# A post-norm attention and ternary-FFN layer: a new hand-written order of the instruction queues, PSUM banks open to every stage, and a last pair whose FFN runs one batch at a time

## The chip, the cores and the metric

The kernel runs on one core of a Trainium2 chip. The metric is device time in microseconds (us) of that core. Each engine (TensorE = PE, VectorE = DVE, ScalarE = ACT, GpSimd = POOL, and SyncE = SP, which issues the DMAs) runs its own list of instructions strictly in the order in which they are written. Engines meet only at semaphores.

## The reference

For 32 batches of 256 tokens of width 128 (fp32 throughout):

```
Q, K, V = x Wq^T, x Wk^T, x Wv^T            # 8 heads; Q, K of width 64, V of width 128 per head
A = softmax(Q K^T)                          # no scale, over the 256 keys, per batch and head
x1 = layernorm(x + sum over heads of A V)
h = silu((x1 w1^T) s1) * ((x1 w2^T) s2)     # 128 -> 512, w ternary times 8
h = gelu((h h1^T) s3); h = gelu((h h2^T) s4)   # 512 -> 512, twice, exact gelu
out = layernorm(x1 + (h w3^T) s5)           # 512 -> 128
```

## The kernel before, in words

**Precision.** Each fp32 operand is split into a high and a low part of the PE's faster fp32r type; a product is three matmuls (high*high, high*low, low*high). The high part is a copy (ACT `copy`, DVE or POOL `tensor_copy`), the low part a subtraction (`minus`, L196). The FFN weights are ternary, so their low parts are zero and two matmuls are enough. That isn't assumed: all low parts of the FFN weights are reduced to one flag, PE reads it (L1101) and branches to a body with or without the third matmul. The traced run takes the body without it.

**Tiling.** Two batches make a pair of 512 tokens; there are 16 pairs. One matmul writes up to one PSUM bank of 512 fp32 columns; there are 8 banks. A pair needs:

- `query_or_key(i, t)`, t = 0..7, and `values(i, n)`, n = 0..7: three 512-wide matmuls each. ACT copies the high part out of the bank (`t_high`, `v_high`), DVE subtracts the low part (`t_low`, `v_low`).
- `scores(i, g)`, g = 0..7: two heads of one batch, 12 matmuls of 64 rows and 256 columns, of which two at a time run side by side. DVE takes the row maximum (`row_max`, L600), ACT the exponential (`exp`, L383, two instructions and two reads of the sum for each of 16 blocks u), DVE the reciprocal, POOL normalizes (`norm`, L248).
- `turn_prob(i, u)`, u = 0..15: four 128x128 transposes (L852) of block u; then `pt_high` on ACT, `pt_low` on DVE; then `times_v(i, u)`, six 256-wide matmuls into bank 7. After the eight blocks of a batch come `acc_copy` (ACT), `turn_attention` (two transposes), `res_add`, `stats`, `norm1` (DVE) and `rstd` (POOL).
- FFN: `turn_x1` (four transposes), `layer1_z1`/`layer1_z2`, o = 0..3 (two 512-wide matmuls each), `tanh` (ACT), `silu` and `gate` (DVE); `layer2`, `layer3` (32 512-wide matmuls each, in halves of four per output), each output through `gelu2`/`gelu3` (ACT), `high` and `low`; `layer4` (8 matmuls), `yt_copy`, `turn_y`, `y_add`, `stats2`, `rstd2`, `norm2`, store.

**Staging.** `cycle(k)` (L989) is the PE's order of one period. It is written out by hand and mixes three pairs: it ends the FFN of pair k-2, does most of the attention of pair k and the FFN of pair k-1, and starts Q, K, V and scores of pair k+1. ACT, DVE and POOL have hand-written loops over k with the same period. Cycles 0 to 18 all run the same text; where a pair doesn't exist the call does nothing. Cycle 0 comes after a short prologue, and the flag is read after it.

**Banks.** Every stage has fixed banks (L22 to L32): Q, K, V in banks 2 and 4, all transposes of probabilities in bank 3, FFN in 0 and 1, scores in 5 and 6, the sum over heads in 7. Before PE writes a bank again it waits for the last reader; those waits are the extra tuples of each call in `cycle`.

**The head.** SP issues x^T of pair 0, all weights, the residual of pair 0 and then (L216) x^T of pair 1, which needs the buffer `xt_in` free. ACT and DVE split Wq, Wk, Wv; POOL splits the 11 pieces of the FFN weights between the `norm`s of cycle 0 (`split_weights`), DVE reduces each (`largest_lo`, L558), PE turns the maximum (`turn_flag`), DVE makes the flag (L570).

**The tail.** The FFN of pair 15 runs in cycles 16 and 17, where no other pair is left.

**ACT's function tables.** The exponential and tanh are in one table, gelu in another; a copy works with both. Where the order goes from `exp` or `tanh` to `gelu` or back, an ACT_TABLE_LOAD stands in ACT's queue. Per pair the order of before has four groups of gelu: `gelu3(k-2,3)` with `gelu3(k-2,2)` before it, `gelu2(0,1)`, `gelu2(2,3)`, `gelu3(0,1)`.

The change also touches every function that names a bank.

Of the kernel before, what the change touches and what calls it, by code (L numbers as in the profile page):

```python
# [21 lines left out]
T_BANK = (2, 2, 4, 4, 2, 4, 2, 2)  # L22
V_BANK = (4, 2, 4, 4, 2, 4, 2, 4)
TURN_BANK = (3, 3, 3, 3, 3, 3, 3, 3, 3, 3, 3, 3, 3, 3, 3, 3)
AT_BANK = (2, 4)
X1T_BANK = 1
Z1_BANK = (0, 0, 0, 1)
Z2_BANK = (1, 1, 0, 0)
L2_BANK = (1, 0, 1, 0)
L3_BANK = (1, 0, 1, 0)  # L30
L4_BANK = 1
YT_BANK = 1  # L32

T_FIRST = {0: 0, 1: 1, 2: 2, 3: 4, 4: 0, 5: 1, 6: 2}
V_FIRST = {0: 4, 1: 0, 2: 1, 3: 2}
# [5 lines left out]
def need(eng, sem, value):  # L41

    if value > 0:
        eng.wait_ge(sem, value)


def layer_kernel(nc, x, x_t, wq_t, wk_t, wv_t, w1_t, w2_t, h1_t, h2_t, w3_t, scales_t, out):
# [8 lines left out]
    VT = TT * H * D // TOK  # L56

# [6 lines left out]
    def after(i, per, n):  # L64

        return min(i * per + n, PAIRS * per)

    with ExitStack() as ctx:
# [38 lines left out]
        with ExitStack() as early:  # L107
# [26 lines left out]
        sc = bank[5:7]  # L134
# [3 lines left out]
        (s_wqk, s_wv, s_wf, s_ident, s_wqk_hi, s_wqk_lo, s_wv_hi, s_wv_lo, s_wf_hi, s_wf_lo, s_lomax,  # L138
         s_flagt, s_flag, s_zero, s_scales, s_halves, s_held) = (sem(n) for n in (
            "wqk_in", "wv_in", "wf_in", "ident_made", "wqk_hi", "wqk_lo", "wv_hi", "wv_lo", "wf_hi", "wf_lo",  # L140
            "lomax_made", "flag_turned", "flag_made", "zeroed", "scales_in", "halves_ready", "held"))
# [19 lines left out]
        WF = [(w1_hi[:, :], w1_lo[:, :], w1_in[:, :]), (w2_hi[:, :], w2_lo[:, :], w2_in[:, :])]  # L161
        WF += [(h1_hi[:, c, :], h1_lo[:, c, :], h1_in[:, c, :]) for c in range(KC)]
        WF += [(h2_hi[:, c, :], h2_lo[:, c, :], h2_in[:, c, :]) for c in range(KC)]
        WF += [(w3_hi[:, :, :], w3_lo[:, :, :], w3_in[:, :, :])]
        NWF = len(WF)
# [7 lines left out]

        def v_cols(n):
            t, half = V_ORDER[n]
            return t, slice(half * TOK, (half + 1) * TOK)

        def t_bank(i, t):
            return bank[T_FIRST[t] if i == 0 and t in T_FIRST else T_BANK[t]]

        def v_bank(i, n):
            return bank[V_FIRST[n] if i == 0 and n in V_FIRST else V_BANK[n]]

# [3 lines left out]
        def slot(i, u, ring):  # L187
            return (i * J + u) % ring
# [13 lines left out]
        def _(sp):  # L202
            sp.dma_start(xt_in[:, :], x_t[0]).then_inc(s_xin, 16)
            sp.dma_start(wq_in[:, :], wq_t).then_inc(s_wqk, 16)
            sp.dma_start(wk_in[:, :], wk_t).then_inc(s_wqk, 16)
            sp.dma_start(wv_in[:, :], wv_t).then_inc(s_wv, 16)
            sp.dma_start(scales[:, :], scales_t).then_inc(s_scales, 16)
            sp.dma_start(w1_in[:, :], w1_t).then_inc(s_wf, 16)
            sp.dma_start(w2_in[:, :], w2_t).then_inc(s_wf, 16)
            sp.dma_start(h1_in[:, :, :], h1_t.rearrange("(c p) o -> p c o", p=P)).then_inc(s_wf, 16)  # L210
            sp.dma_start(h2_in[:, :, :], h2_t.rearrange("(c p) o -> p c o", p=P)).then_inc(s_wf, 16)
            sp.dma_start(w3_in[:, :, :], w3_t.rearrange("(c p) o -> p c o", p=P)).then_inc(s_wf, 16)
# [17 lines left out]
            for k in range(-3, PAIRS + 3):  # L230
                load_res(k)
                load_xt(k + 3)
                store(k - 2)
            sp.wait_ge(s_yfree, 16 * PAIRS)

        @block.gpsimd
        def _(pool):
# [26 lines left out]
            def split_weights(k, g):  # L264
                if k == 0:
                    hi, lo, w = WF[g]
                    if g == 0:
                        pool.wait_ge(s_wf, 16 * 5)
                    nc.gpsimd.tensor_copy(hi, w).then_inc(s_wf_hi, 1)
                    pool.wait_ge(s_wf_hi, g + 1)  # L270
                    minus(nc.gpsimd, lo, w, hi).then_inc(s_wf_lo, 1)

            def low(f, layer, c):
                if there(f):
                    full, hi, lo, _, s_hi, s_lo = LAYER[layer]
                    pool.wait_ge(s_hi[c], f + 1)
                    minus(nc.gpsimd, lo[:, c, :], full[:, c % 2, :], hi[:, c, :]).then_inc(s_lo[c], 1)

# [14 lines left out]

            def norm2(f):
# [6 lines left out]

            norm(0, 0)
            norm(0, 1)
            norm(0, 2)

            for k in range(PAIRS + 3):
                low(k - 2, 3, 2)
                rstd1_of(k - 1, 1)
                norm(k, 3)
                split_weights(k, 0)  # L310
                norm(k, 4)
                split_weights(k, 1)
                norm(k, 5)
                split_weights(k, 2)
                norm(k, 6)
                split_weights(k, 3)
                norm(k, 7)
                split_weights(k, 4)
                low(k - 1, 1, 0)
                norm(k, 8)  # L320
                split_weights(k, 5)
                norm(k, 9)
                split_weights(k, 6)
                low(k - 1, 1, 1)
                norm(k, 10)
                split_weights(k, 7)
                low(k - 1, 1, 2)
                norm(k, 11)
                split_weights(k, 8)
                norm(k, 12)  # L330
                split_weights(k, 9)
                low(k - 1, 2, 0)
                low(k - 1, 2, 1)
                norm(k, 13)
                split_weights(k, 10)
                low(k - 1, 2, 2)
                norm(k, 14)
                rstd2_of(k - 2)
                norm(k, 15)
                low(k - 1, 3, 0)  # L340
                norm(k + 1, 0)
                rstd1_of(k, 0)
                norm(k + 1, 1)
                norm(k + 1, 2)

        @block.scalar
        def _(act):
# [4 lines left out]
            def split_wv(g):  # L352
                cols = slice(g * TOK, (g + 1) * TOK)
                if g == 0:
                    act.wait_ge(s_wv, 16)
# [788 lines left out]
```

## Time and profile before

| | |
|---|---|
| median of 3 runs | 1031.53 us (1029.31 to 1032.75) |
| the profiled execution | 1031.28 us, of which the span from first to last instruction is 1029.4 us |
| PE busy | 984.3 us (96%) |
| PE weight load busy | 816.5 us (79%) |
| ACT busy | 859.1 us (83%) |
| DVE busy | 827.1 us (80%) |
| POOL busy | 513.0 us (50%) |
| mean granted TensorE clock | 0.98 of full speed |

The profile shows one execution. A matmul's row starts when it starts; its end is modelled and overlaps the next one's start, so the pace of PE is read from start to start, not from the durations. "Idle before" is the idle time of an engine ahead of a group, with the instruction that ended it.

### The profile page before, as it was taken

What the parts mean: (1) busy time and instruction counts of PE and PEld (TensorE: products, weight loads), DVE (VectorE), ACT (ScalarE), POOL (GpSimd) and SP (SyncE); (2) the same over time, 40 slices, a digit from 0 to 9 for tenths busy, and PEclk for the clock granted to TensorE, in tenths of its full rate; (3) what the DMA queues carried; (4) which work ended last, traced back from release to release, by engine and by line L of the source; (5) the groups of instructions that cost most, each with busy time, mean ns of one, the idle gap of its engine ahead of it and who ended that gap; (6) DMA issues with size and microseconds to landing.
All of it is one profiled execution on the core that took longest, in us unless ns stands there. A gap on an engine that the chain in (4) does not pass through costs nothing.

```text
span 1029.4 us, 19535 instructions
## 1 busy us (share of the span) xinstructions
PE 984.3 (96%) x6465; PEld 816.5 (79%) x6465; DVE 827.1 (80%) x1827; ACT 859.1 (83%) x1992; POOL 513.0 (50%) x509
## 2 busy tenths in 40 slices
PE   4887999999999999999999999999999999999976
PEld 3676888888888888888888888888888888888844
DVE  4695778887888988788898878889887888878754
ACT  5574998989899898989989898998989899898632
POOL 1591545544455554545555454555545454554623
PEclk9898999999999999999999999999999999999978
DMA  5000000000100000010000001000000100000000
GB/s 184 11 3 21 2 11 12 21 11 2 31 2 22 12 21 11 1 32 2 21 12 21 12 2 32 2 22 11 22 11 2 32 1 12 11 12 11 12 0 21
DMA packets 21749, 17.81 MB, mean 17 GB/s; under 512 B 1040, under 2 KB 17936, under 8 KB 21648
## 3 DMA queue, kind: packets, MB, share of 16 engines
q1 hardware_dynamic: 21648, 16.53, 5.3%
q8 instruction: 56, 0.92, 0.4%
q14 instruction: 45, 0.37, 0.1%
HBM read 12.33 MB, written 4.19 MB: 16 GB/s over the span
## 4 chain that ended last, share of the span: by engine, by line
PE 91%; DVE 4%; ACT 2%; issue 2%; DMA 0%; POOLq 0%; SPq 0%; DVEq 0%; POOL 0%; ACTq 0%
PE bank L852 13%; PE bank L958 13%; PE bank L959 13%; PE bank L846 12%; PE bank L848 11%; PE bank L847 11%; PE bank L891 11%; PE bank L938 3%; PE bank L939 3%; ACT prob L383 1%; DVE pt_lo L196 1%; DMA wk_in<-in_wk_t 0%; DVE neg_max L600 0%; DVE t_lo L196 0%; DVE v_lo L196 0%
## 5 line engine op out<-in xcount | busy, mean ns | idle before, releaser
L248 POOL TENSOR_TENSOR prob<-prob,inv_total 128x512 f32<-128x512 f32 x256 | 267.8, 1057 | 185.0 <-DVE inv_total L606 185.0
L383 ACT ACTIVATE prob<-bank,neg_max 128x256 f32<-128x256 f32 x512 | 237.9, 480 | 4.1 <-DVE neg_max L600 3.4
L196 DVE TENSOR_TENSOR pt_lo<-bank,pt_hi 128x512 fp32r<-128x512 f32 x256 | 175.4, 685 | 46.3 <-ACT pt_hi L199 41.8
L199 ACT ACTIVATE pt_hi<-bank 128x512 fp32r<-128x512 f32 x256 | 154.2, 602 | 66.9 <-PE bank L852 64.5
L600 DVE TENSOR_REDUCE neg_max<-bank 128x2 f32<-128x512 f32 x256 | 171.4, 681 | 24.7 <-PE bank L891 24.7
L852 PE MATMUL bank<-ident,prob 128*128 128x128 f32 x1024 | 157.7, 277 | 7.2 <-issue 4.7
L852 PEld LDWEIGHTS bank<-ident,prob 128*128 128x128 f32 x1024 | 120.9, 141 | 39.9 <-issue 9.6
L846 PE MATMUL bank<-pt_hi,v_hi 128*128 128x256 f32 x512 | 151.9, 297 | 0.0
L848 PE MATMUL bank<-pt_hi,v_lo 128*128 128x256 f32 x512 | 145.3, 284 | 0.0
L847 PE MATMUL bank<-pt_lo,v_hi 128*128 128x256 f32 x512 | 145.3, 284 | 0.0
L196 POOL TENSOR_TENSOR even_lo<-gelus,even_hi 128x512 fp32r<-128x512 f32 x48 | 61.8, 1288 | 103.7 <-DVE even_hi L678 103.7
L383 ACT ACTIVATION_READ_ACCUMULATOR prob<-bank,neg_max 128x1 f32 x512 | 108.3, 212 | 0.0
L958 PE MATMUL bank<-odd_hi,h_hi 128*128 128x512 f32 x256 | 107.0, 418 | 0.0
L958 PE MATMUL bank<-even_hi,h_hi 128*128 128x512 f32 x256 | 105.6, 412 | 0.2 <-DVE even_lo L196 0.2
L196 DVE TENSOR_TENSOR v_lo<-bank,v_hi 128x512 fp32r<-128x512 f32 x128 | 86.9, 679 | 23.1 <-ACT v_hi L199 23.1
L196 DVE TENSOR_TENSOR t_lo<-bank,t_hi 128x512 fp32r<-128x512 f32 x128 | 86.9, 680 | 19.5 <-ACT t_hi L199 19.5
L847 PEld LDWEIGHTS bank<-pt_lo,v_hi 128*128 128x128 f32 x512 | 98.3, 192 | 4.3
L959 PE MATMUL bank<-odd_lo,h_hi 128*128 128x512 f32 x256 | 101.5, 397 | 0.0
L846 PEld LDWEIGHTS bank<-pt_hi,v_hi 128*128 128x128 f32 x512 | 98.1, 192 | 4.0
L959 PE MATMUL bank<-even_lo,h_hi 128*128 128x512 f32 x256 | 101.1, 395 | 0.0
L848 PEld LDWEIGHTS bank<-pt_hi,v_lo 128*128 128x128 f32 x512 | 98.3, 192 | 0.0
L199 ACT ACTIVATE v_hi<-bank 128x512 fp32r<-128x512 f32 x128 | 77.2, 603 | 23.7 <-PE bank L848 23.7
(101 smaller groups left out, 2357.2 us busy)
## 6 DMA issues: line engine op xcount, KB each, us to landing
xt_in<-in_x_t SPq DMA_DIRECT2D x16, 256.0 KB, 2.7
res<-in_x SPq DMA_DIRECT2D x16, 256.0 KB, 2.8
out_x<-y SPq DMA_DIRECT2D x16, 256.0 KB, 2.3
h_in<-in_h_t SPq DMA_DIRECT2D x2, 1024.0 KB, 9.2
w_in<-in_w_t SPq DMA_DIRECT2D x3, 256.0 KB, 5.9
wv_in<-in_wv_t SPq DMA_DIRECT2D x1, 512.0 KB, 5.9
wq_in<-in_wq_t SPq DMA_DIRECT2D x1, 256.0 KB, 3.1
wk_in<-in_wk_t SPq DMA_DIRECT2D x1, 256.0 KB, 5.1
```

The lines of the kernel that those rows point to most:

```text
L196: return eng.tensor_tensor(dst, src, hi.bitcast(F32), ALU.subtract)
L199: return nc.scalar.activation(dst, src, ACT.Copy)
L248: nc.gpsimd.tensor_tensor(prob[:, s, :, :], prob[:, s, :, :], inv_total[:, u, :].unsqueeze(2).to_broadcast([P, NT, N]), ALU.mult).then_inc ...
L383: last = nc.scalar.activation(prob[:, slot(i, u, RING), nt, :], sc[u % 2][:, nt * N:(nt + 1) * N], ACT.Exp, bias=neg_max[:, u, nt:nt + 1], ...
L600: nc.vector.tensor_reduce(neg_max[:, u, :], sc[u % 2].rearrange("p (t m) -> p t m", m=N), AX.X, ALU.max, negate=True).then_inc(s_max, 1)
L846: mm(dst, w_hi, m_hi, start=start, stop=False)
L847: mm(dst, w_hi, m_lo, start=False, stop=False)
L848: return mm(dst, w_lo, m_hi, start=False, stop=stop)
L852: last = turn(dst[:, n * P:(n + 1) * P], b, ident[:, :])
L891: ends.append(mm(sc[n][:, nt * N:(nt + 1) * N], left[rows, t, q], right[rows, t + 1, m], start=(term == 0), stop=(term == 2)))
L958: mm(dst, w_hi[:, c, cols], m_hi[:, c, :], start=begins, stop=False)
L959: last = mm(dst, w_hi[:, c, cols], m_lo[:, c, :], start=False, stop=ends and not with_lo)
```

## The change

1. **Banks.** The tables of fixed banks are replaced by tables in which every stage may use banks 0 to 6; scores get a pair of banks for each g (`SC_BANK`) in place of banks 5 and 6. Tables `*_OTHER` override them for the pairs 0, 1, 13, 14 and 15. `scores` waits for named readers in place of the fixed wait on `exp` of the scores before.
2. **The order of a pair.** `cycle(k)` and the loops of ACT, DVE and POOL are written in a new order, used for k = 1 to 14. The work of a pair is the same, but for three moves: the copy `xt_high(k+2)` goes from ACT to POOL, `high(k-1,2,0)` from DVE to ACT, `low(k-1,2,1)` from POOL to DVE. All eight `query_or_key` of pair k+1 and its `scores` 0 to 2 are now in cycle k. On ACT the gelus of a pair stand in two groups.
3. **The first pairs.** Prologue and cycle 0 become one list of its own on each engine. Wq and Wk are loaded in two parts each (128 and 384 columns), with a semaphore for each load; the splits are spread over ACT, DVE and POOL; POOL splits the FFN weights earlier. On ACT `xt_high(1)` stands after `t_high(0,3)`. The flag is read when `turn_prob(0,14)` has been issued.
4. **The last pair.** `last` replaces cycles 15 to 18. It runs the FFN of pair 15 as two batches of 256 columns each: every 512-wide matmul becomes two 256-wide ones, every evacuation two of half the width, with semaphores `s_ends` of their own. The chunks of layers 2 to 4 are interleaved between the batches. Store and final norm go by batch as well.

```diff
-T_BANK = (2, 2, 4, 4, 2, 4, 2, 2)
-TURN_BANK = (3, 3, 3, 3, 3, 3, 3, 3, 3, 3, 3, 3, 3, 3, 3, 3)
-Z1_BANK = (0, 0, 0, 1)
-L2_BANK = (1, 0, 1, 0)
+T_BANK = (2, 0, 3, 0, 1, 5, 6, 3)
+SC_BANK = ((4, 2), (5, 6), (3, 1), (3, 5), (1, 6), (1, 3), (3, 2), (1, 5))
+TURN_BANK = (2, 0, 4, 2, 4, 4, 1, 6, 0, 3, 6, 3, 0, 4, 0, 6)
+AT_BANK = (1, 0)
+L2_BANK = (2, 4, 0, 1)
...
             sp.dma_start(xt_in[:, :], x_t[0]).then_inc(s_xin, 16)
-            sp.dma_start(wq_in[:, :], wq_t).then_inc(s_wqk, 16)
-            sp.dma_start(wk_in[:, :], wk_t).then_inc(s_wqk, 16)
+            sp.dma_start(wq_in[:, A], wq_t[:, A]).then_inc(loads["wqa"], 16)
+            sp.dma_start(wk_in[:, A], wk_t[:, A]).then_inc(loads["wka"], 16)
+            sp.dma_start(wq_in[:, B_], wq_t[:, B_]).then_inc(loads["wqb"], 16)
+            sp.dma_start(wk_in[:, B_], wk_t[:, B_]).then_inc(loads["wkb"], 16)
...
# ACT, first pairs
+            weight_high("wka")
+            t_high(0, 0)
+            t_high(0, 1)
+            t_high(0, 2)
+            weight_high("wv1")
+            t_high(0, 3)
+            xt_high(1)
+            weight_high(0)
+            t_high(0, 4)
+            t_high(0, 5)
+            exp(0, 0)
+            exp(0, 1)
...
# ACT, the gelus of a pair in the loop over k
+                gelu3(k - 2, 2)
+                gelu3(k - 2, 3)
...
+                gelu2(k - 1, 0)
+                high(k - 1, 2, 0)
+                pt_high(k, 11)
+                gelu2(k - 1, 1)
+                gelu2(k - 1, 2)
+                t_high(k + 1, 5)
+                t_high(k + 1, 6)
+                t_high(k + 1, 7)
+                gelu2(k - 1, 3)
...
+                gelu3(k - 1, 0)
+                gelu3(k - 1, 1)
+                v_high(k + 1, 3)
...
# PE, one stretch of cycle(k)
+                turn_prob(k, 9, (s_t_lo, k + 1, H, 3))
+                query_or_key(k + 1, 4, (s_exp, k, J, 15))
+                turn_prob(k, 10, (s_v_lo, k + 1, VT, 3))
+                layer2(k - 1, 2, 0, w, (s_t_lo, k + 1, H, 4))
                 layer2(k - 1, 0, 1, w)
+                turn_attention(k, 0, (s_t_lo, k + 1, H, 5))
+                turn_prob(k, 11, (s_pt_lo, k, J, 10))
                 layer2(k - 1, 1, 1, w)
+                layer2(k - 1, 3, 0, w, (s_radd, k, 2, 1))
+                layer2(k - 1, 2, 1, w)
+                query_or_key(k + 1, 5, (s_exp, k, J, 16))
+                scores(k + 1, 0, (s_gelu2, k - 1, KC, 2), (s_gelu2, k - 1, KC, 1))
...
# a chunk of a layer of the last pair, one batch
+            def quarter(b, c, dst, w_hi, w_lo, m_hi, m_lo, cols, with_lo, prior, s_out, readers):
+                m = of_batch(b)
+                free(*readers)
+                pe.wait_ge(*half_done(prior, 1, b, c))
+                begins, ends = c == 0, c == KC - 1
+                mm(dst, w_hi[:, c, cols], m_hi[:, c, m], start=begins, stop=False)
+                last = mm(dst, w_hi[:, c, cols], m_lo[:, c, m], start=False, stop=ends and not with_lo)
...
# PE, the end of last(w)
+                times_v(15, 13)
+                turn_x1_half(0, (s_yadd, 14, 1, 1))
+                times_v(15, 14)
+                times_v(15, 15)
+                layer1_z1_half(0, 0, w, (s_yt, 14, 1, 1))
+                turn_attention(15, 1, (s_x1t_lo, 15, 1, 1))
+                layer1_z1_half(0, 1, w, (s_radd, 15, 2, 1))
+                layer1_z2_half(0, 0, w, (s_acc, 15, 2, 2))
...
+                turn_y_half(0, (s_gelu3, 15, KC, 2))
+                layer4_half(1, 2, w)
+                layer4_half(1, 3, w)
+                turn_y_half(1, (s_gelu3, 15, KC, 5))
```

## Rows read from the trace of the kernel before

**Rows 1.** Stretches: length, busy time (instructions) by engine, PE clock, DMA share, GB/s.

```profile
0.00:40.00 40.00, 22.56 (x101) 16.43 (x102) 19.53 (x35) 19.63 (x48) 9.50 (x16) 0.87 0.38 125
40.00:77.90 37.90, 33.90 (x259) 27.33 (x257) 34.20 (x75) 28.30 (x85) 31.62 (x34) 1.00 0.02 8
82.20:144.92 62.72, 60.66 (x388) 50.67 (x388) 44.88 (x94) 50.88 (x121) 27.76 (x27) 0.93 0.04 10
398.49:458.65 60.16, 60.16 (x406) 50.50 (x406) 50.83 (x114) 54.33 (x125) 30.85 (x31) 1.00 0.05 14
927.00:980.90 53.90, 53.18 (x360) 44.78 (x359) 43.12 (x98) 41.42 (x96) 28.67 (x28) 1.00 0.04 11
980.90:1029.40 48.50, 31.86 (x112) 20.68 (x110) 24.14 (x57) 12.92 (x20) 14.30 (x14) 0.79 0.04 11
```

**Rows 2.** Timeline of PE in one pair: start, duration, engine, line, tiles, count.

```profile
402.59 0.39 PE L939 MATMUL bank<-x1t_lo,w_hi 128*128 128x512 f32 x1
402.82 0.60 PE L852 MATMUL bank<-ident,prob 128*128 128x128 f32 x4
403.17 0.48 PE L938 MATMUL bank<-x1t_hi,w_hi 128*128 128x512 f32 x1
403.49 0.40 PE L939 MATMUL bank<-x1t_lo,w_hi 128*128 128x512 f32 x1
403.81 0.39 PE L891 MATMUL bank<-t_hi 64*128 64x256 f32 x2
404.03 0.28 PE L891 MATMUL bank<-t_lo,t_hi 64*128 64x256 f32 x2
...
404.51 0.28 PE L891 MATMUL bank<-t_hi,t_lo 64*128 64x256 f32 x2
404.72 0.50 PE L938 MATMUL bank<-x1t_hi,w_hi 128*128 128x512 f32 x1
405.06 0.39 PE L939 MATMUL bank<-x1t_lo,w_hi 128*128 128x512 f32 x1
...
406.31 0.28 PE L847 MATMUL bank<-pt_lo,v_hi 128*128 128x256 f32 x1
406.43 0.28 PE L848 MATMUL bank<-pt_hi,v_lo 128*128 128x256 f32 x1
...
409.74 0.63 PE L852 MATMUL bank<-ident,prob 128*128 128x128 f32 x4
410.30 0.39 PE L891 MATMUL bank<-t_hi 64*128 64x256 f32 x2
```

**Rows 3.** Groups by line in that pair: count, busy, mean ns, idle before.

```profile
L383 ACT ACT_TABLE_LOAD x4 | 5.1, 1283 | 0.1
L383 ACT ACTIVATE prob<-bank,neg_max 128x256 f32<-128x256 f32 x32 | 14.9, 481 | 0.0
L199 ACT ACTIVATE pt_hi<-bank 128x512 fp32r<-128x512 f32 x16 | 9.6, 603 | 3.2 <-PE bank L852 3.1
L196 DVE TENSOR_TENSOR pt_lo<-bank,pt_hi 128x512 fp32r<-128x512 f32 x17 | 11.7, 686 | 2.6 <-ACT pt_hi L199 2.3
```

**Rows 4.** Timeline of the head; in brackets, idle before and what ended it.

```profile
8.79 0.79 PE L846 MATMUL bank<-xt_hi,wq_hi 128*128 128x512 f32 x1 [8.79 <-DVE wk_lo L196]
8.91 21.33 SPq L218 DMA_DIRECT2D xt_in<-in_x_t  x2
...
82.23 1.09 PE L852 MATMUL bank<-ident,prob 128*128 128x128 f32 x4 [4.72 <-issue]
```

**Rows 5.** The loads of `xt_in` in the first 60 us, from issue to landing.

```profile
DMA to landing us min/median/max: 2.7/2.9/8.3
```

**Rows 6.** Timeline of the tail, in the same form.

```profile
982.22 0.42 DVE L621 TENSOR_TENSOR res<-bank,res 128x256 f32<-128x256 f32 x1 [0.69 <-PE bank L852]
...
1021.29 0.63 PE L852 MATMUL bank<-ident,yt 128*128 128x128 f32 x4 [0.87 <-ACT yt L446]
1021.96 0.69 DVE L690 TENSOR_TENSOR y<-bank,x 128x512 f32<-128x512 f32 x1 [2.33 <-PE bank L852]
```

More of the change, by code:

```diff
@@ L172, in layer_kernel, with half_done, of_batch @@
         }
+        s_ends = {n: (sems(f"end{n}_hi"), sems(f"end{n}_lo")) for n in (1, 2, 3)}
+        def half_done(layer, low, b, c):
+            return (s_ends[layer][low][c], 1) if b else (LAYER[layer][4 + low][c], LAST + 1)
+        def of_batch(b):
+            return slice(b * N, (b + 1) * N)
         def v_cols(n):
@@ L467, in _ @@
+            exp(0, 4)
             v_high(0, 2)
+            exp(0, 5)
             v_high(0, 3)
-            xt_high(1)
-            for k in range(PAIRS + 3):
+            pt_high(0, 1)
+            pt_high(0, 2)
+            exp(0, 6)
+            exp(0, 7)
+            pt_high(0, 3)
+            t_high(1, 0)
+            exp(0, 8)
+            v_high(0, 4)
+            t_high(1, 1)
+            v_high(0, 5)
+            exp(0, 9)
+            pt_high(0, 4)
+            pt_high(0, 5)
+            v_high(0, 6)
@@ new lines, in _ @@
+            xt_high(2)
+            v_high(0, 7)
+            exp(0, 10)
+            exp(0, 11)
+            exp(0, 12)
+            pt_high(0, 6)
+            t_high(1, 2)
+            t_high(1, 3)
+            exp(0, 13)
+            pt_high(0, 7)
+            pt_high(0, 8)
+            exp(0, 14)
+            v_high(1, 0)
+            t_high(1, 4)
+            weight_high(6)
+            exp(0, 15)
+            pt_high(0, 9)
+            pt_high(0, 10)
+            acc_copy(0, 0)
+            exp(1, 0)
@@ L472, in _ @@
+            v_high(1, 1)
+            exp(1, 1)
+            t_high(1, 5)
+            pt_high(0, 11)
+            pt_high(0, 12)
+            v_high(1, 2)
+            t_high(1, 6)
+            exp(1, 2)
+            exp(1, 3)
+            pt_high(0, 13)
+            t_high(1, 7)
+            pt_high(0, 14)
+            exp(1, 4)
+            pt_high(0, 15)
+            v_high(1, 3)
+            for k in range(1, LAST):
                 pt_high(k, 0)
+                gelu3(k - 2, 2)
                 gelu3(k - 2, 3)
-                t_high(k, 7)
@@ new lines, in _ @@
+            row_max(1, 1)
+            pt_low(0, 10)
+            inverse(0, 14)
+            largest_low(6)
+            v_low(1, 1)
+            largest_low(7)
+            t_low(1, 5)
+            pt_low(0, 11)
+            pt_low(0, 12)
+            largest_low(8)
+            t_low(1, 6)
+            v_low(1, 2)
+            row_max(1, 2)
+            largest_low(9)
+            row_max(1, 3)
+            largest_low(10)
+            res_add(0, 0)
+            flag_by_partition()
+            halves()
@@ new lines, in _ @@
+            high(14, 1, 3)
+            low(14, 1, 2)
+            inverse(15, 13)
+            row_max(15, 15)
+            stats2_of(13)
+            pt_low(15, 9)
+            high(14, 2, 0)
+            low(14, 2, 0)
+            low(14, 2, 1)
+            v_low(15, 6)
+            low(14, 2, 2)
+            high(14, 2, 3)
+            low(14, 2, 3)
+            v_low(15, 7)
+            inverse(15, 14)
+            pt_low(15, 10)
+            res_add(15, 0)
+            high(14, 3, 0)
+            inverse(15, 15)
@@ L1100, in _ @@
+            times_v(0, 11)
+            scores(1, 1, (s_pt_lo, 0, J, 13), (s_t_lo, 1, H, 6))
+            scores(1, 2, (s_exp, 1, J, 2), (s_t_lo, 1, H, 7))
+            turn_attention(0, 0, (s_v_lo, 1, VT, 3))
+            values(1, 3, (s_pt_lo, 0, J, 12))
+            times_v(0, 12)
+            query_or_key(1, 7, (s_exp, 1, J, 3))
+            turn_flag((s_radd, 0, 2, 1))
+            turn_prob(0, 14, (s_exp, 1, J, 4))
+            pe.wait_ge(s_halves, 2)
             pe.wait_ge(s_flag, 1)
```

1454 lines of the change are left out of this document (1085 added, 369 removed).

## Prediction

> **What bounds the kernel now.** I read the table of stretches first, then PE's own timeline, then ACT's groups, then the two ends of the span.
>
> In the middle PE is the bound and nothing else comes near. From 398.49 to 458.65, one period of 60.16 us, PE is busy for all of it, ACT for 54.33, DVE for 50.83 and POOL for 30.85 [rows 1]. PE's waits in the middle (120 to 930) are an empty list. So the middle can only get shorter if the same matmuls take PE less time. The ends are different. Ahead of 77.9 DVE is busy for 19.53 + 34.20 = 53.7 us and ACT for 47.9; PE is idle until 8.79, and the clock of the first 40 us is 0.87 [rows 1, 4]. The last 48.5 us hold 31.86 us of PE at a clock of 0.79 [rows 1].
>
> Score block 0 of a pair is transposed once a period, and I cut the span there. Those places are 144.92 for pair 2 and 927.00 for pair 15. The span is then: PE's work until the flag, which ends at 82.23 - 4.72 = 77.5; an idle stretch of 4.7 for reading the flag and branching [rows 4]; 62.7 to the start of pair 2; 13 x 60.16 = 782.1; a tail of 53.9 + 48.5 = 102.4 [rows 1]. Sum 1029.4. The profiled execution took 1031.28, 1.9 more than its span, and the median of the runs is 1031.5.
>
> **PE's price list.** Start to start, a 512-wide matmul takes 0.23 (402.59 to 402.82), a 256-wide one 0.12 (406.31 to 406.43, and a side-by-side pair of scores likewise), four transposes 0.35 (402.82 to 403.17). The matmul behind transposes takes 0.32, 0.09 more. Going into scores costs 0.09 on the matmul before and 0.10 on the first scores (403.49, 403.81, 404.03), 0.19; leaving them costs 0.09 and 0.11 (404.51, 404.72, 405.06), 0.20. Transposes ahead of scores take 0.56 in place of 0.35 (409.74 to 410.30), with the 0.10 that is 0.31 [rows 2]. Scores into transposes isn't in the rows: between 0.09 and 0.20, I take 0.15.
>
> A pair has 136 512-wide matmuls, 96 + 48 slots of 256, and 76 transposes: at 0.232, 0.119 and 0.089 that is 31.6 + 17.1 + 6.8 = 55.5. Before, 16 matmuls follow transposes (1.4); scores are entered six times from a matmul and twice from transposes (1.76) and left five times to a matmul and three times to transposes (1.45). Sum 60.1, against 60.16 measured: the list closes, and there is no hidden stall in the middle.
>
> **The new order of a pair.** It has the same instructions on PE. 16 matmuls still follow transposes. Scores are entered six times from a matmul, once from transposes, and once from scores (`scores(k+1,1)` and `(k+1,2)` are neighbours); left five times to a matmul and twice to transposes. That is 1.45 + 1.30 against 1.76 + 1.45: 0.46 less, so 59.7.
>
> Would PE now wait? Gelus stand in two groups, not four, so four of the eight table loads go (the four to the exponential in rows 3, and as many to gelu), 4 x 1.283 = 5.1 us of ACT per pair [rows 3]; the copy that goes to POOL and the one that comes from DVE cancel (0.6 each). ACT falls to about 49 of 59.7. DVE trades a copy for a subtraction (0.686), about 51. POOL gets a copy (0.6) and loses a subtraction. By the orders, the PE time between `scores` and the transposes of its blocks is 13.6 us at the least, before 13.2; between a transpose and its `times_v` 3.8, before 2.4. The tightest place is bank 1: `turn_attention(k,0)` writes it and `layer2(k-1,3,0)` takes it again after 1.4 us (0.36 + 1.02), when `res_add` has read it. DVE has `pt_low(k,10)` ahead of `res_add`, and ACT has `pt_high(9)`, `t_high(4)`, `exp(15)`, `pt_high(10)` ahead of that: from the end of `turn_prob(k,9)` 0.6 + 0.6 + 0.96 + 0.6 on ACT [rows 3], 0.69 and 0.42 on DVE [rows 3, 6] and some 0.3 for semaphores, 4.2. PE's own work until there is 0.79 + 0.36 + 1.02 + 0.93 + 0.18 + 0.36 + 1.02 = 4.7. It fits by 0.5. I add 0.1 per pair for places that don't: 59.8, at the least 59.6, at the most 62.3 (a miss of one exp, one copy and one subtraction, 2.3, on top of 60). 13 pairs give 777.4, 4.7 less than before.
>
> **The head.** The small first parts of Wq and Wk should let PE start near 5.5 in place of 8.79 [rows 4]: x^T comes first as before, a copy and a subtraction follow, and 64 KB come sooner than 256. I count nothing for it. ACT now has `xt_high(1)` fifth in its list, ahead of the first exponentials. x^T of pair 1 was issued at 8.91 behind all weights and landed 8.3 later, at 17.2 [rows 4, 5]; nothing moves it up. So ACT stands still from about 11 to 17 and DVE behind it. Before, `exp(0,0)` began before 17; now it begins near 19.5. What is won is the rest: by the flag ACT has to do about 42.5 us (before 47.9; it has three `pt_high`, two `exp` and three weight copies fewer), some 3 of them before 17; DVE about 52 (before 53.7), some 7 before 17. POOL, busy for 31.6 of 37.9 us up to the flag [rows 1] since it began on the weights only in cycle 0, now begins them at once. DVE is the bound: 17 + 45 = 62 if it never waits. From 40 to 77.9 it waited 10% of the time [rows 1]; with 5.5 us of waits PE's work until the flag ends at 67.5. It can't be under 62; if the blocks of ACT and POOL cost as much as the old order's waits did it is 77.5. I take 67.5. The 4.7 us of the branch stay. Cycle 1 was 62.7 for 56.7 us of PE work by the list, the rest being a cold clock (0.93, rows 1) and one more gap; the new cycle 1 has 55.8 with the one transposition group before it, so 61.8. Pair 2 starts at 67.5 + 4.7 + 61.8 = 134.0, 10.9 earlier.
>
> **The tail.** From the transposes of block 0 of pair 15, PE has 76.0 us of work in the old order and 76.4 in the new (a 256-wide matmul costs 0.119, half of 0.232, so the halves add 0.5). Behind PE's last transposes comes the chain of norm and store: 1021.29 to 1029.4, 8.1 us [rows 6]; for half the tokens I take 6 (between 5 and 8). Before, 102.4 - 76.0 - 8.1 = 18.3 us were stalls and a cold clock, all but one of them in the FFN of pair 15, which ran alone. Now batch 0 starts its FFN when 14 of 16 `times_v` are out, and each batch hides the other's evacuations. A chain remains for batch 1: `turn_attention`, residual, norm, `turn_x1` take some 7 us, as before, but beside batch 0; then four outputs per layer, each with gelu, copy, subtraction, 2.5 to 3 us a layer for three layers. Against it stand 24 us of PE work. I take 8.5 us of stalls (between 4 and 15) in place of 18.3. Tail 76.4 + 6 + 8.5 = 91, 11.4 less.
>
> The Trainium skill, "TensorE: Matmul & The Clock Gate", section "Back-to-back issue gap", speaks against the halves: in a stream of weight load and matmul pairs it gives 81 ns at 128 columns and 131 ns at 512, so that halving the columns doesn't halve the time; an estimate from it for 256 is 98, which would make the 88 FFN matmuls of the last pair 5.7 us dearer. This case's trace doesn't agree: 0.12 at 256 columns and 0.23 at 512 [rows 2], 0.5 us for all of them.
>
> **Sum.** 67.5 + 4.7 + 61.8 + 777.4 + 91 = 1002.4 us of span, with 1.9 around it 1004.3; against the median (0.3 above the profiled execution) 1004.5. I say 1004, 2.7% faster.
>
> **Rivals.**
> - *The middle gains nothing.* Small bank waits eat the 0.46 a pair and 0.1 to 0.6 more. For it: margins of 0.5 us, 69 bank reuses per pair, none of which the old trace shows. Against: ACT gets 5 us of air. 13 x 0.4 to 1.0 more: 1009 to 1017. 17%.
> - *The head gains nothing.* The wait for x^T of pair 1 on ACT costs more than POOL's early start gives, and the flag comes at 77 as before. For it: the 6 us in which ACT stands. 1014. 13%.
> - *Both ends are better than I think.* DVE waits under 3 us behind 17, the tail has under 5 us of stalls: 995. 17%.
> - *The other side: one wait per pair in the middle.* The DVE queue is late at bank 1 because `exp(k,15)` or a table load falls ahead of `pt_high(k,10)`; the stall of PE comes once each pair. It decides from (1031.5 - 1004.5) / 14 = 1.9 us a pair; with 2.4 (one load, one copy and the subtraction late) it is 1004.5 + 14 x 2.4 = 1038. For it: strict queues, margin 0.5. Against: distances to the transposes grew nearly everywhere. 7%.
> - *The order doesn't do what it says*, because the clock stays low in the head: it is in the numbers above. 1%.
> - My forecast, 999 to 1009: 45%.
>
> **How the numbers follow.** The forecast, the better ends and most of the first two rivals lie between 991 and 1018; what is left out is the other side and their far tails, 2 in 10. About 0.3% is what a measurement of this kernel can tell. Faster by that: 0.46 + 0.17 + 0.13 + 0.14 = 0.90; within it 0.03; slower 0.07.
>
> **What would show it.** Right: a period of 59.6 to 60.0 between the transposes of block 0, PE busy throughout, four table loads a pair; ACT idle ahead of `xt_high(1)` until 17; the flag read near 67; the last transposes of PE 85 us behind those of block 0 of pair 15. Wrong: a releaser of PE in the middle with a total over 10 us; the flag later than 75; a tail over 97.

## The result and the profile after

The changed kernel takes 1008.36 us (median of 4 runs, 1007.14 to 1008.57); the kernel before took 1030.72 in the same series (4 runs, 1029.31 to 1032.75). The ratio is 0.9774, with a 95% interval of 0.9762 to 0.9786: 2.3% faster. The forecast was 1004 with a range of 991 to 1018.

I cut the span after at the same places as before: where PE's work ends at the flag, where it goes on, the transposes of score block 0 of pair 2 (now at 129.81) and of pair 15 (now at 918.83). The table of stretches of the changed kernel, in the columns of [rows 1]:

```profile
0.00:64.30 64.30, 50.97 (x357) 42.26 (x357) 48.75 (x101) 44.02 (x129) 39.69 (x47) 0.92 0.25 79
64.30:69.49 5.19, 0.00 (x1) 0.03 (x1) 3.86 (x13) 1.70 (x6) 5.11 (x5) 0.72 0.18 43
69.49:129.81 60.32, 59.33 (x389) 50.76 (x390) 47.46 (x97) 47.27 (x119) 23.80 (x26) 0.94 0.04 12
129.81:918.83 789.02, 777.32 (x5253) 658.34 (x5252) 712.82 (x1469) 648.48 (x1574) 383.80 (x390) 1.00 0.05 14
918.83:1006.50 87.67, 79.16 (x557) 69.86 (x555) 70.01 (x171) 55.96 (x133) 49.76 (x55) 0.97 0.05 13
```

| part | before | forecast | after |
|---|---|---|---|
| PE's work until the flag | 77.5 | 67.5 | 64.3 |
| idle ahead of the branch's program | 4.7 | 4.7 | 5.2 |
| to the start of pair 2 | 62.7 | 61.8 | 60.3 |
| 13 pairs | 782.1 | 777.4 | 789.0 |
| tail | 102.4 | 91 | 87.7 |
| span | 1029.4 | 1002.4 | 1006.5 |

Both ends gave more than forecast, 29.8 us with the idle time and cycle 1 in place of 22.3. The middle, which was to give 4.7, took 6.9. Together that is the 22.9 by which the spans differ. Its 13 periods are 60.69 us each in place of 60.16 [rows 1], although the 777.32 us of PE's work in them is 59.79 a pair. The missing 0.90 has a single place. The waits of the middle, where the list of PE was empty before (one row: who waited <- for what, us in total, times, longest):

```profile
PE bank L1455 <- DVE x L982: 11.7, 13, 0.9
```

It is `turn_x1`, which turns the normed tokens of the pair before for the FFN. First what DVE and POOL did ahead of it, then PE's own row:

```profile
141.40 0.71 POOL L369 TENSOR_TENSOR rstd<-var_eps,minus_half 128x2 f32<-128x2 f32 x1
141.59 0.67 DVE L260 TENSOR_TENSOR pt_lo<-bank,pt_hi 128x512 fp32r<-128x512 f32 x1
142.09 3.04 POOL L327 TENSOR_TENSOR prob<-prob,inv_total 128x512 f32<-128x512 f32 x3
142.17 3.29 DVE L982 TENSOR_SCALAR x<-res,mv,rstd 128x128 f32<-128x128 f32 x4
145.52 0.66 PE L1455 MATMUL bank<-ident,x 128*128 128x128 f32 x4 [0.90 <-DVE x L982]
```

The four operations that write `x` (`norm1` of both batches) take 3.29 us, and beside the first three of them POOL runs three norms of `prob` back to back; the fourth begins when POOL is done and takes 0.33 again. In the kernel before, the same four stood in a gap between two norms:

```profile
454.51 2.04 POOL L248 TENSOR_TENSOR prob<-prob,inv_total 128x512 f32<-128x512 f32 x2
...
456.48 1.11 DVE L645 TENSOR_SCALAR x<-res,mv,rstd 128x128 f32<-128x128 f32 x4
...
458.34 1.04 POOL L248 TENSOR_TENSOR prob<-prob,inv_total 128x512 f32<-128x512 f32 x1 [1.79 <-DVE inv_total L606]
```

Over the middle, one line for each kernel, before and then after (shortest, median and longest of 52, in ns):

```profile
L645 DVE TENSOR_SCALAR x<-res,mv,rstd x52: 333/342/448, 155.7 to 878.4; 128x128 f32<-128x128 f32 x52
```

```profile
L982 DVE TENSOR_SCALAR x<-res,mv,rstd x52: 333/1056/1079, 142.2 to 873.4; 128x128 f32<-128x128 f32 x52
```

So the same instruction on the same shapes is three times as long. The trace of before held the effect already, at a place where nobody waited: four operations of `norm2`, of the same shape and also from SBUF to SBUF (the on-chip memory that isn't PSUM), start at 200.76, and the last of them, the only one beside a norm of POOL (from 201.40), takes 1.06 us where the others take 0.34. Over the middle of before:

```profile
L697 DVE TENSOR_SCALAR y<-y,mv,rstd x52: 331/337/1062, 200.8 to 922.8; 128x128 f32<-128x128 f32 x52
```

The length of `x` is what the page's chain of waits shows too: its line "DVE x L982 5%" is the only one of DVE in it above 1%, because the chain runs through `x` once a pair.

The head, in the form of [rows 4]. ACT stands in front of `xt_high(1)`, PE waits for a subtraction that is behind it, and the branch comes at 64:

```profile
17.96 0.63 ACT L263 ACTIVATE xt_hi<-xt_in 128x512 fp32r<-128x512 f32 x1 [7.21 <-DMA xt_in<-in_x_t]
20.41 0.58 PE L1498 MATMUL bank<-t_hi 64*128 64x256 f32 x2 [7.40 <-DVE t_lo L260]
63.68 0.62 PE L1455 MATMUL bank<-ident,prob 128*128 128x128 f32 x4
69.49 1.94 PE L1455 MATMUL bank<-ident,prob 128*128 128x128 f32 x8 [5.20 <-POOL prob L327]
```

The tail, answering to [rows 6]. The last transposes of PE start at 1000.52, 81.7 behind those of block 0 of pair 15, and the stores of the two halves are issued at 1002.86 and after:

```profile
974.50 0.44 PE L1455 MATMUL bank<-ident,at 128*128 128x128 f32 x2 [0.24 <-ACT at L263]
977.57 0.36 PE L1627 MATMUL bank<-odd_hi,h_hi 128*128 128x256 f32 x1 [0.98 <-DVE odd_lo L260]
1000.52 0.44 PE L1455 MATMUL bank<-ident,yt 128*128 128x128 f32 x2 [0.57 <-ACT yt L639]
1002.86 1.78 SPq L299 DMA_DIRECT2D out_x<-y  x2
```

### The profile page after: what moved, and what is told of

The parts are those of the page before. It is cut to its first block, busy times and chain, and to the rows that moved or that the text cites. A ratio compares the mean times of both kernels' runs of the same rounds, so it can differ in the third digit from the quotient of the medians.

```text
span 1006.5 us, 19738 instructions
## 1 busy us (share of the span) xinstructions
PE 966.8 (96%) x6553; PEld 821.3 (82%) x6553; DVE 882.9 (88%) x1846; ACT 797.4 (79%) x1958; POOL 502.2 (50%) x520
## 4 chain that ended last, share of the span: by engine, by line
PE 86%; DVE 8%; issue 2%; POOL 1%; DMA 1%; SPq 1%; ACT 1%; POOLq 0%; DVEq 0%; ACTq 0%
PE bank L1567 13%; PE bank L1568 12%; PE bank L1455 12%; PE bank L1449 11%; PE bank L1451 11%; PE bank L1450 10%; PE bank L1498 10%; DVE x L982 5%; PE bank L1547 3%; PE bank L1548 3%; DVE y L1027 1%; DMA xt_in<-in_x_t 1%; DVE res L958 1%; DVE stats L964 1%; PE bank L1627 1%
## 5 line engine op out<-in xcount | busy, mean ns | idle before, releaser
L327 POOL TENSOR_TENSOR prob<-prob,inv_total 128x512 f32<-128x512 f32 x256 | 272.3, 1072 | 179.2 <-DVE inv_total L943 179.2
L1449 PE MATMUL bank<-pt_hi,v_hi 128*128 128x256 f32 x512 | 158.2, 309 | 0.0
L1455 PEld LDWEIGHTS bank<-ident,prob 128*128 128x128 f32 x1024 | 123.3, 142 | 30.1 <-POOL prob L327 5.4
L260 POOL TENSOR_TENSOR odd_lo<-gated,odd_hi 128x512 fp32r<-128x512 f32 (+1 forms) x50 | 62.2, 1244 | 83.5 <-ACT odd_hi L263 82.9
L1567 PE MATMUL bank<-even_hi,h_hi 128*128 128x512 f32 x240 | 98.8, 412 | 0.0
L1567 PE MATMUL bank<-odd_hi,h_hi 128*128 128x512 f32 x240 | 97.3, 405 | 0.0
L263 ACT ACTIVATE t_hi<-bank 128x512 fp32r<-128x512 f32 x128 | 76.3, 598 | 23.7 <-PE bank L1451 19.5
L1568 PE MATMUL bank<-odd_lo,h_hi 128*128 128x512 f32 x240 | 94.8, 395 | 0.0
```

Of the source, the lines that this page charges most:

```text
L260: return eng.tensor_tensor(dst, src, hi.bitcast(F32), ALU.subtract)
L263: return nc.scalar.activation(dst, src, ACT.Copy)
L327: nc.gpsimd.tensor_tensor(prob[:, s, :, :], prob[:, s, :, :], inv_total[:, u, :].unsqueeze(2).to_broadcast([P, NT, N]), ALU.mult).then_inc ...
L1449: mm(dst, w_hi, m_hi, start=start, stop=False)
L1455: last = turn(dst[:, n * P:(n + 1) * P], b, ident[:, :])
L1567: mm(dst, w_hi[:, c, cols], m_hi[:, c, :], start=begins, stop=False)
```

## Experiments

All are edits of the changed kernel (1008.36). Each was timed against the kernel before; times below are medians, ratios are to the kernel before with 95% intervals. For comparison, the changed kernel has 0.9774 [0.9762, 0.9786].

**POOL keeps still while `x` is written (e1_pool_waits)**

```diff
                 rstd1_of(k - 1, 1)
+                hold(pool, s_x1, 2 * k)
                 norm(k, 5)
```

> One wait more on POOL: behind rstd1 of batch 1 it waits for the two norm1 of that pair (four tensor_scalars of x) before it goes on with the norm of score block 5. Theory A (the four tensor_scalars of x are slow because POOL's norms of prob run beside them): L982 falls from a mean of 1056 ns to about 340, x is ready some 2.9 us sooner, PE's 0.90 us wait for x ahead of turn_x1 is gone from every pair, the period goes from 60.69 to about 59.8; 13 periods and the last pair give about 12 us: 996 (994 to 999). Rival B (they are slow by themselves, in the place or the operands that the new order gives them): L982 stays above 1000 ns, the wait of PE stays 0.9, 1008. Rival C (A's gain is given back because POOL's norms come some 1.5 us later and the transposes of block 5 wait for them): L982 at 340 ns, but a new wait of PE for POOL of about 1 us per pair, 1005 to 1010.

Measured: 995.71 us (994.88 to 996.74), ratio 0.9653 [0.9637, 0.9669]. The stretch from block 0 of pair 2 to that of pair 15 is wholly PE's work, 59.75 a period, and `x` is fast again:

```profile
128.71:905.44 776.73, 776.73 (x5253) 659.29 (x5252) 687.22 (x1469) 648.01 (x1574) 384.77 (x390) 1.00 0.05 14
```

```profile
L983 DVE TENSOR_SCALAR x<-res,mv,rstd x52: 334/339/344, 141.1 to 858.9; 128x128 f32<-128x128 f32 x52
```

```profile
141.09 1.10 DVE L983 TENSOR_SCALAR x<-res,mv,rstd 128x128 f32<-128x128 f32 x4
142.12 0.68 DVE L260 TENSOR_TENSOR pt_lo<-bank,pt_hi 128x512 fp32r<-128x512 f32 x1
142.37 3.04 POOL L327 TENSOR_TENSOR prob<-prob,inv_total 128x512 f32<-128x512 f32 x3 [1.34 <-DVE x L983]
```

POOL waits 1.34 us for `x` and then takes the same 3.04 for its three norms, and nobody waits for it in turn: PE has no wait at all in the middle. Theory A holds, B and C fall. One added wait is worth 12.7 us.

**The first half of `norm1` earlier (e2_norm1_split)**

```diff
                 y_add(k - 2)
+                norm1(k - 1, 0)
                 inverse(k, 5)
                 inverse(k, 6)
                 inverse(k, 7)
                 pt_low(k, 2)
-                norm1(k - 1, 0)
                 norm1(k - 1, 1)
```

> Only the order of DVE is changed: norm1 of batch 0 comes directly behind the addition into y, ahead of three reciprocals and a subtraction (pt_low of block 2). Theory A (the length of the x operations beside POOL is the cause, not their place): L982 stays between 700 and 1056 ns, but two of the four are out before, so x is ready 1 to 2 us sooner; PE's wait for x shrinks to 0 to 0.3 and the time to 996 to 1001, if the delayed subtraction of block 2 doesn't become a wait of its own (then a new row of PE for pt_lo, and 1003 to 1010). Rival B (x is late because rstd of batch 1 is late on POOL, wherever norm1 of batch 0 stands): the wait stays 0.9, 1008.

Measured: 996.63 us (995.95 to 998.17), ratio 0.9664 [0.9648, 0.968]. PE's wait for `x` is gone from all pairs of the middle. The median of the `x` operations is lower than the 700 to 1056 that I had given, because most of the first two now fall ahead of POOL's norms; only the longest is what it was:

```profile
L982 DVE TENSOR_SCALAR x<-res,mv,rstd x52: 340/462/1079, 140.9 to 860.3; 128x128 f32<-128x128 f32 x52
```

The time agrees with theory A, the length of the operations doesn't; rival B falls. Two edits on two engines that both take operations of `x` from beside POOL's norms give the same 12 us.

**Eight table loads a pair in place of four (e5_more_loads, e10_loads_in_gaps)**

The first puts them between the gelus, the second where ACT waited longest:

```diff
+            def extra_switch():
+                nc.scalar.activation(junk[:, :], scales[:, 0:1], ACT.Exp)
...
                 gelu3(k - 2, 2)
+                extra_switch()
                 gelu3(k - 2, 3)
...
                 gelu2(k - 1, 1)
+                extra_switch()
                 gelu2(k - 1, 2)
```

```diff
+            def extra_switch():
+                nc.scalar.activation(junk[:, :], scales[:, 0:1], ACT.Gelu)
...
                 v_high(k, 4)
+                extra_switch()
                 x1t_high(k - 1)
...
                 exp(k + 1, 2)
+                extra_switch()
                 pt_high(k, 13)
```

> Each of the two groups of gelus in a pair is cut in two by an exponential of one column into a scratch tile, so that ACT loads its tables eight times per pair as before the change, not four. Theory A (in the middle PE bounds, ACT's 49 us of a 60.7 us period leave room, and the four loads that the change saves are worth nothing by themselves): ACT busy near 54 us per period, period within 0.3 of 60.7, 1008 to 1012. Rival B (grouping the gelus is what keeps the ring of banks moving): PE gets waits for gelu2, gelu3 or the next exponentials of 1 to 3 us per pair, 1022 to 1048.

> The same four extra table loads per pair as in e5_more_loads, but placed where ACT of the changed kernel waits longest: a gelu of one column into the scratch tile ahead of x1t_high (ACT waits 1.38 us there) and ahead of pt_high of block 13 (it waits 1.07 there and 0.58 at the next copy). Theory A (the 33 us of e5_more_loads come from its place, 2.8 us between two gelus with scores' blocks queued behind; ACT's total has room, 55 of 60.7): the lump overhangs each gap by about 1.4, which the distances of 3 us and more between a copy and its reader take up; 1008 to 1016. Rival B (a lump of 2.8 us on ACT costs PE about its overhang wherever it stands, so the four loads that the grouping saves are worth 1 to 3 us per pair): 1022 to 1048.

Measured: 1041.41 us (1040.0 to 1043.11), ratio 1.0097 [1.008, 1.0113], and 1039.63 us (1039.44 to 1040.68), ratio 1.0092 [1.0077, 1.0108]. Theory A was wrong both times, by 29 and 24 us from the upper end of its ranges, and B was right. ACT is busy for 55.37 and 55.27 us of a period, with over 7 us to spare, and yet both periods are long, 63.19 and 62.97. PE's waits in the middle, of the first and then of the second:

```profile
PE bank L1504 <- ACT prob L539: 15.1, 12, 1.5
PE bank L1504 <- DVE t_lo L261: 13.4, 12, 1.1
PE bank L1461 <- DVE x L988: 10.8, 12, 0.9
```

```profile
PE bank L1461 <- ACT prob L539: 11.8, 24, 0.6
PE bank L1461 <- DVE x L988: 10.8, 12, 0.9
PE bank L1573 <- DVE pt_lo L261: 6.0, 12, 0.5
```

Besides the wait for `x` that was there already, a lump of 1.28 + 0.2 + 1.28 us makes PE wait 1.1 and 1.3 on average at two places when it stands between the gelus, and 0.5 at each of three places when it stands in ACT's widest gaps. (In the second, 0.8 us of the longer period isn't in these rows, because a matmul's modelled end hides the first part of a wait. Read from start to start beside the changed kernel, in one period, PE loses 0.73, 0.57 and 0.74 us at the three places and 0.06 to 0.08 at each of three matmuls behind the first, 2.2 of the 2.3.) So this order, which all but fills PE, has no distance left for two loads in one lump at these places, where ACT's total would have had room. That grouping the gelus is a condition for the rest of the change isn't shown by this: the order of before has eight loads a pair, one by one, and PE waits for nothing in its middle. A new order with the loads spread like that was not run.

**The last pair like all others (e4_old_tail)**

```diff
-            load_res(15)
-            store(13)
-            store(14)
-            store_half(0)
-            store_half(1)
...
-                for k in range(1, LAST):
+                for k in range(1, PAIRS + 2):
                     cycle(k, False)
-                last(False)
```

The lists of the last pair go from all engines, and with them the bank tables of their own from pair 13 on; counts are cut off at the last pair as they were before the change.

> The last pair goes as all others do: pair 15 in the steady order, then its layers for both batches at once, one store; the head and the order of the middle stay. Theory A (the tail's 14.7 us come from running the last layers one batch at a time, so that one batch's matmuls cover the other's gelus, copies and subtractions): the tail from the transposes of score block 0 of pair 15 is 100 to 103 us again in place of 87.7, and the time 1021 to 1024. Rival B (most of the tail's gain comes from the new order of a pair, which the last pair shares): the tail is 88 to 93, 1009 to 1014. Between the two, each us of the tail is a us of the time.

Measured: 1019.88 us (1019.05 to 1020.96), ratio 0.9886 [0.987, 0.9903]. The time is 1.1 below A's range, but the tail is as A said: block 0 of pair 15 is at 915.05, so it takes 102.65 us, as much as before the change (102.4) and 15.0 more than with the list of the last pair.

```profile
915.05:1017.70 102.65, 83.75 (x469) 66.61 (x467) 70.88 (x153) 51.48 (x111) 45.27 (x45) 0.92 0.04 11
```

None of the tail's gain comes from the new order of a pair. It all comes from the list of the last pair, whose parts (the halves by batch, the place of the last `times_v`, the banks of pairs 13 to 15) this edit takes out together; PE's waits in the tail are 2.5 us with the list and 11.3 without it, and the mean clock is 0.97 and 0.92. The other 3.8 us, by which this kernel came to pair 15 sooner, lie in the head: 0.6 ahead of the flag, an idle time of 4.14 in place of 5.20, and a clock that was soon back:

```profile
67.87 1.14 PE L1169 MATMUL bank<-ident,prob 128*128 128x128 f32 x8 [4.14 <-issue]
```

Eight transposes take 1.14 us here and 1.94 in the changed kernel. From 64 to 80 the mean granted clock is 0.89 here and 0.68 there. The instructions up to there are the same. Why the idle time is 1.06 shorter wasn't tested; the program behind the branch is another one here.

**The loads of x^T of pair 1 and who stands behind them (e3_xt_late, e7_xt_early)**

The first moves the copy that waits, on ACT; the second moves the transfer, on SP:

```diff
-            xt_high(1)
             weight_high(0)
             t_high(0, 4)
             t_high(0, 5)
             exp(0, 0)
             exp(0, 1)
+            xt_high(1)
```

```diff
             sp.dma_start(scales[:, :], scales_t).then_inc(s_scales, 16)
...
+            load_xt(1)
             sp.dma_start(w1_in[:, :], w1_t).then_inc(loads["w1"], 16)
...
-            load_xt(1)
             load_xt(2)
```

> Only ACT's order in the head is changed: the copy xt_high(1), which waits for x^T of pair 1 until 17.96, goes from its place ahead of weight_high(0) to behind exp(0,1). Theory A (that wait at the head of ACT's strict queue holds back what PE, DVE and POOL do next, and what is behind it is worth its own length): one weight copy, two copies of t and two exponentials, some 3.6 us of ACT, are done before 17.96; the flag comes 2.5 to 4 us sooner and the time is 1004.5 (1004 to 1006). Rival B (the 7 us in which ACT stands are covered, since the head is bound by DVE's sum of work): the flag comes at 64 as before, 1007.5 to 1009.

> Only SP's order is changed: the load of x^T of pair 1 is issued behind the scales, ahead of w1, w2, h1, h2, w3 and the residual; it still waits for the first x^T to be used up (4.9 us), so the loads behind it are issued about 1 us later. Theory A (the transfer's place is what makes ACT stand from 10.75 to 17.96): it lands at 8 to 10, ACT doesn't wait, PE's idle 7.4 us before 20.41 go nearly all, and the flag comes 4 to 6.5 us sooner: 1003 (1001.5 to 1005). Rival B (the time moves on: w1 and h1, h2 come later, and POOL, ACT or DVE then wait for them): the flag gains under 2 us, 1006.5 to 1009.

Measured: 1003.49 us (1002.54 to 1005.12), ratio 0.974 [0.9726, 0.9753], and 999.29 us (998.35 to 999.95), ratio 0.9694 [0.9681, 0.9707]. A holds in both, and both gains are above A's best: the flag comes at 58.56 and 55.08 in place of 63.95. With the early transfer ACT takes `xt_high(1)` without a wait:

```profile
11.15 0.62 ACT L263 ACTIVATE xt_hi<-xt_in 128x512 fp32r<-128x512 f32 x1
```

What I had left out is the clock. First the changed kernel, then the one with the early transfer, for the first 40 us:

```profile
0.00:40.00 40.00, 26.68 (x155) 21.05 (x156) 25.40 (x51) 23.42 (x67) 22.28 (x31) 0.87 0.39 126
```

```profile
0.00:40.00 40.00, 33.70 (x241) 27.50 (x242) 33.52 (x69) 31.68 (x92) 30.90 (x39) 1.00 0.39 126
```

The idle 7.4 us ahead of 20.41 cost their length and then PE's slow clock behind them: from 20.41 to 26.00 it is 0.53 in the changed kernel, and scores whose rows show 0.28 at 10.66 and again at 26.16 show 0.45 at 20.76. At that clock 5.6 us do the work of 3.0, an estimate of 2.6 us lost; with the 6.6 by which the idle time shrank (7.4 to 0.8) that is 9.2, against 9.1 measured.

**The branch (e6_no_branch, e11_read_only)**

```diff
-            any_lo = pe.value_load(lo_flag[0:1, 0:1].bitcast(I32))
-            with pe.If(any_lo):
...
-            with pe.Else():
-                rest_of_first(False)
+            rest_of_first(False)
...
```

The first has neither the wait for the flag, nor the reading, nor the branch; the second keeps wait and reading.

> Leaves out the test of the weights at run time: PE reads no flag and has no branch, only the program that the flag chooses here (without the low parts of the five FFN weights). Theory A (the 5.2 us ahead of the transposes of block 15 of pair 0 are the reading and the branch): they go, and the clock of the first microseconds behind them is back, 1002.5 (1001 to 1003.5). Rival B (POOL works for 5.11 of those 5.2 us, so PE would soon wait for POOL's norms and low parts in their place): a new wait of PE for POOL of 2 to 4 us near 66, 1005 to 1007.

> Leaves out the branch but keeps the wait for the flag and its reading into a register of PE; the program is the one that the flag chooses here (without the low parts of the five FFN weights). e6_no_branch, with neither, is 6.4 us faster than the changed kernel. Theory A (the jump into another part of the program, whose instructions have to be fetched, is most of the 5.2 us of idle PE and so of the slow clock behind it): 1002 to 1004. Rival B (reading a value from memory into a register of PE is most of it): 1006 to 1008.5.

Measured: 1001.96 us (1001.65 to 1003.53), ratio 0.9726 [0.9713, 0.9739], and 1001.51 us (1000.46 to 1003.06), ratio 0.9719 [0.9706, 0.9733]. Between these two there is no difference that the runs can tell; the second is half a us below A's range. The reading costs nothing that can be measured, the branch 6.4 to 6.9 us by the medians and 5 to 6 by the ratios. Both edits take out the jump and the body that isn't run together. The idle time explains half of it: without the branch PE goes on at 66.21 in place of 69.49, and has a wait of 1.86 for an exponential there.

```profile
66.21 1.06 PE L1455 MATMUL bank<-ident,prob 128*128 128x128 f32 x8 [1.86 <-ACT prob L538]
```

The rest is the clock: its mean from 64 to 80 is 1.00 in e6_no_branch, 0.89 in e11_read_only and 0.68 with the branch, where it is 0.50 from 69.49 to 76.78; at half the clock 7.3 us, less half a us in which PE stood, lose some 3.4, an estimate. The length of the idle time alone doesn't decide the clock behind it: e11_read_only has the same idle 1.86 as e6_no_branch, and its eight transposes take 1.83 us at a mean clock of 0.54 (66.16 to 68.00), where e6_no_branch has 1.06 us at 1.00.

```profile
66.16 1.83 PE L1455 MATMUL bank<-ident,prob 128*128 128x128 f32 x8 [1.86 <-ACT prob L538]
```

The releaser that the trace names at 69.49, a norm of POOL, is thus not the cause; PE's own branch was. The Trainium skill ("Runtime: NRT & Kernel Launch", "Instruction fetch mechanics") says that a taken branch outside the part of the program already fetched has to wait for a transfer of instructions; these runs agree with it in that only the branch costs. The trace has two packets of the kind "instruction", 0.03 MB together, between 64.30 and 66.5 with the branch, and none between 64.3 and 66.21 in e6_no_branch. Whose instructions they are it doesn't say, and PE goes on only 3 us behind them, so that the wait is for this transfer isn't shown.

**Both repairs together (e8_hold_early)**: the edits of e1_pool_waits and e7_xt_early.

> The changed kernel with POOL's wait for the two norm1 and the early load of x^T of pair 1 together. Theory A (a wait in each pair of the middle and a wait in the head have nothing to do with each other, the gains add): 995.7 less 5, 991 (989 to 993). Rival B (the head's gain is eaten in pair 0 or 1 by something else): 994 to 996.

Measured: 986.04 us (985.38 to 987.03), ratio 0.9565 [0.9552, 0.9578]: 2.2% faster than the changed kernel and 4.3% faster than the one before. 12.7 and 9.1 below 1008.4 would be 986.6, so the gains add, as theory A said. The time lies 3 us below its range because the range counted 5 us for the early load, which alone had given 9.1.

```profile
120.81:897.54 776.73, 776.73 (x5254) 659.27 (x5253) 687.16 (x1469) 648.03 (x1574) 384.83 (x390) 1.00 0.05 14
```

## Why the prediction was right, and where it wasn't

The time lies in the range, and the forecast of 1004 missed by 4.4 us. That it came so near is in part luck: against the forecast the 13 pairs are 11.6 us longer, and the two ends with the idle time are 7.5 shorter. The bound (PE in the middle) and the gain of both ends were right as mechanisms; the middle was not. One of the signs named for "wrong", a releaser of PE in the middle with a total over 10 us, is there with 11.7.

- **The list of PE's prices and the saved transitions** were right. "0.46 less, so 59.7": with PE never waiting, the period is 59.75 (e1_pool_waits and e8_hold_early).
- **"I add 0.1 per pair for places that don't"** is the step that failed. Measured is 0.90 per pair, 11.7 us of waits, at a place that I hadn't priced. I looked for the tightest place where banks are reused, and took DVE's durations from the rows of before as if they belonged to the instruction. No wait stands at bank 1. The duration of `norm1` belonged to its neighbourhood: 342 ns in a gap of POOL, 1056 beside it. With `x` (and other operations of DVE that grew the same way, see the last section) DVE is busy for 54.8 us a pair, not 51; 2.0 of that is `x`. With PE's wait for `x` the middle came out 0.5 us a pair above before; the case "the middle gains nothing" (17%) came true, by another mechanism than the one that it named.
- **"Four of the eight table loads go"**: right, 58 loads in the whole execution for 116. But I counted them as air for ACT, in a sum. e5_more_loads and e10_loads_in_gaps show that the distances decide and not the sum. Their 2.5 and 2.3 us per pair are near the 2.4 of the rival of the other side, but by coincidence: that rival had DVE late at bank 1, and these waits stand at other places.
- **The head**: ACT's stall, forecast from about 11 to 17, was 10.75 to 17.96, and PE started at 5.30 for 5.5. The step was 17 + 45 and 5.5 us of waits, 67.5; it was 64.3. The waits were right and DVE's work was too high:

```profile
17.00:64.30 47.30, 43.26 (x324) 36.58 (x324) 41.86 (x88) 39.62 (x122) 34.59 (x35) 0.91 0.02 7
```

DVE is busy for 41.86 of these 47.30 us, where I had 45, and waits for 5.4; 3.86 us of its work fell into the idle stretch behind 64.30. So the head of the case "both ends are better" came, but not by its DVE waits under 3 us. The rival in which the stall eats the head's gain did not come. The stall cost 9.1 us (e7_xt_early), but of a gain that would have been 22.
- **The branch's** 4.7 were 5.2. What the clock behind them costs was in the measure of cycle 1, and I did not see it as the branch's price: with it the branch costs some 6 us, not 4.7.
- **The tail**: the work of PE behind block 0 of pair 15, the stalls and the last norms were put at 76.4, 8.5 and 6. From the end of PE's last transposes (1000.96) to the end of the span it is 5.5. PE's waits in between are 2.5, and its work takes the other 79.6: 82.1 for the 84.9 of the first two terms. That running the last pair by its own list gains the tail is shown by e4_old_tail; that it is one batch's matmuls beside the other's evacuations fits the waits of both kernels, but no run takes that part out alone. Its stalls were priced too high.

## What to carry to other kernels

A duration taken from a trace holds for what ran beside it: when an order moves a DVE operation from SBUF to SBUF next to a run of POOL's operations, price it at what POOL's take, and look in the trace for the longest of its kind, not only for the median. When one engine is busy without a gap, don't ask whether another has time left in the sum, but how far each of its results is ahead of its reader. And read a stall at its whole price: in these heads the idle times of PE of 7.4 and 5.2 us were each followed by a stretch at a lower clock that cost about 3 us again (2.6 and 3.4, the estimates above).

## What the runs showed of the hardware

- DVE's `tensor_scalar` of 128 x 128 f32 from SBUF to SBUF takes 342 ns, and 1056 ns while POOL runs its `tensor_tensor` of `prob`, whose own length is the same with and without it: a median of 1041 ns in the changed kernel and 1042 in e1_pool_waits. Other DVE operations whose operands are all in SBUF grow too: in the middle of the changed kernel the subtraction `even_lo` takes 1.41 us at 173.77, beside a norm of POOL, and 0.68 at 180.68, beside none. DVE's subtractions that read PSUM (`pt_lo` 659 to 693 ns, `v_lo` 668 to 693 over the middle) don't change beside POOL.

  The Trainium skill ("SBUF — State Buffer", "Who interferes with whom") says that a DVE instruction in a two-port mode, which `tensor_scalar` can enter, contends with GpSimd for a shared pair of ports: whichever issues first holds the pair for the whole instruction, and the other fully blocks. By that, each operation is as long as the POOL operation in its way, and the trace agrees for three of every four: 1056 beside 1041. That `x` is computed in such a mode no row shows.
- Two executions of the same instructions ahead of the flag come out of idle times of 4.14 (e4_old_tail) and 5.20 us (the changed kernel) with eight transposes of 1.14 and of 1.94 us. The mean granted clock of the next 4 us is 0.60 in the first and 0.50 (the lower of the two levels, 1.2 GHz) in the second, and 0.97 (nearly all at 2.4 GHz) and 0.58 in the 4 behind. An idle time of 1.86 us was followed by 1.83 us for the same transposes in e11_read_only and by 1.06 in e6_no_branch, so the length of the idle time alone doesn't decide it.
- This branch of PE, into the second body of a long program, costs about 6 us of the time (6.4 and 6.9 by the medians), the reading of its condition nothing that can be measured.
